# Moving the work between a kernel's stages into its attention loops: output projections, norms, router and gate products batch by batch

## What is computed

```python
x = x + tanh(g_xattn[0]) * L0_xattn(ctx, layernorm(x))   # 8 heads of 64; keys and values from ctx and from x; then Wo
x = x + tanh(g_ffn[0])   * L0_ffn(layernorm(x))          # router, top 2 of 8 experts of 256-1024-256, plus a shared one
x = x + tanh(g_xattn[1]) * L1_xattn(layernorm(x), ctx)   # 16 heads of 16; then Wo and its bias
x = x + tanh(g_ffn[1])   * L1_ffn(layernorm(x))          # gate over 16 experts, their q, k, v mixed into one head,
                                                         # causal attention inside a batch, 16 output projections
```

## Time and profile before

| what | us |
|---|---|
| median of 3 runs (lowest, highest) | 980.82 (979.62, 981.01) |
| the profiled execution, its own time | 984.02 |
| its span, first to last instruction | 982.2 |

### The profile page before, as it was taken

The page is one execution under the profiler, slowest core; times in us unless marked ns, Lnnn a source line. Parts: engine busy times, 40 slices in busy tenths (PEclk is TensorE's granted clock), DMA queues, the critical chain, the costliest instruction groups (busy, mean ns, idle before and its releaser), DMA issues.

```text
span 982.2 us, 14323 instructions
## 1 busy us (share of the span) xinstructions
PE 877.5 (89%) x5152; PEld 619.1 (63%) x5152; DVE 482.8 (49%) x1136; ACT 337.8 (34%) x907; POOL 145.8 (15%) x202
## 2 busy tenths in 40 slices
PE   0699999999997799999999988999999966699978
PEld 0555465555645666699889966667776646355557
DVE  3467666756663331013223248466666651666631
ACT  1244344434434121133322323566666611011110
POOL 3221022022000006000000046122233002000000
PEclk9999999999999789899999998999999975799979
DMA  7400001300000635156555333100000000000001
GB/s 218 160 16 1 16 17 28 102 0 2 1 1 1 207 135 171 50 171 218 190 192 166 114 105 119 82 2 2 2 1 2 2 1 1 0 1 0 0 5 33
DMA packets 37413, 62.21 MB, mean 63 GB/s; under 512 B 4595, under 2 KB 28924, under 8 KB 37092
## 3 DMA queue, kind: packets, MB, share of 16 engines
q1 hardware_dynamic: 35812, 57.68, 17.5%
q0 software_dynamic: 1536, 3.67, 1.2%
HBM read 53.08 MB, written 8.26 MB: 62 GB/s over the span
## 4 chain that ended last, share of the span: by engine, by line
PE 74%; DVE 9%; issue 6%; DMA 5%; ACT 2%; POOL 2%; SPq 1%; ACTq 0%; POOLq 0%; DVEq 0%
PE ps L1480 9%; PE ps L1397 8%; PE ps L1098 7%; PE ps L1158 6%; PE ps L1309 6%; PE ps L1147 5%; PE ps L1144 5%; PE ps L1321 5%; PE ps L1221 5%; DMA OT<-slot_rows 3%; PE ps L1131 3%; PE ps L1178 3%; PE ps L1255 3%; PE ps L1244 3%; PE ps L1419 2%
## 5 line engine op out<-in xcount | busy, mean ns | idle before, releaser
L766 DVE TENSOR_REDUCE negmax<-ps 112x1 f32<-112x375 f32 (+1 forms) x192 | 112.8, 587 | 125.0 <-PE ps L1158 62.5
L1098 PEld LDWEIGHTS ps<-ident,arena 112*125 112x125 f32 (+5 forms) x776 | 106.4, 164 | 91.3 <-issue 44.6
L1098 PE MATMUL ps<-ident,arena 112*125 112x112 f32 (+5 forms) x776 | 115.8, 267 | 23.2 <-POOL arena L380 18.2
L1480 PE MATMUL ps<-arena 128*112 128x384 f32 x256 | 91.3, 501 | 12.8 <-DVE arena L1024 12.8
L637 ACT ACTIVATE arena<-ps,negmax 112x375 f32<-112x375 f32 x128 | 73.5, 574 | 58.0 <-DVE negmax L766 58.0
L609 ACT ACTIVATE OT<-ps,bt 128x128 f32<-128x128 f32 x168 | 48.0, 368 | 113.5 <-PE ps L1309 112.6
L1309 PE MATMUL ps<-OT,arena 128*128 128x128 f32 x672 | 80.9, 280 | 0.2 <-DVE OT L874 0.2
L1309 PEld LDWEIGHTS ps<-OT,arena 128*128 128x128 f32 x672 | 79.2, 197 | 0.6 <-issue 0.6
L1321 PE MATMUL ps<-arena,OT 128*128 128x256 f32 x336 | 75.8, 379 | 0.0
L1158 PE MATMUL ps<-arena 128*112 128x487 f32 x128 | 65.9, 598 | 7.0 <-issue 5.1
L534 ACT ACTIVATE arena<-ps,negmax 112x487 f32<-112x487 f32 x64 | 42.7, 667 | 82.7 <-DVE negmax L766 82.6
(11 more groups left out here) (219 smaller groups left out, 1247.2 us busy)
## 6 DMA issues: line engine op xcount, KB each, us to landing
arena<-in_up_w SPq DMA_DIRECT2D x21, 1024.0 KB, 5.1
arena<-in_down_w SPq DMA_DIRECT2D x8, 1024.0 KB, 11.3
arena<-in_wqkv SPq DMA_DIRECT2D x1, 3072.0 KB, 12.5
arena<-in_ctx SPq DMA_DIRECT2D x8, 375.0 KB
slot_rows<-acc SPq DMA_DIRECT2D x3, 896.0 KB, 9.4
OT<-slot_rows SPq DMA_DIRECT2D x21, 128.0 KB, 4.9
slot_out<-yo SPq DMA_DIRECT2D x21, 128.0 KB, 1.7
wbuf<-in_ctxT SPq DMA_DIRECT2D x5, 375.0 KB, 5.3
```

Source lines behind the costliest of these rows:

```text
L766: dve.tensor_reduce(negmax[0:TQ, h % 2:h % 2 + 1], ps[0:TQ, h % 2, 0:n], AX, ALU.max, negate=True)\
L1098: return pe.transpose(dst, src, ident[0:k, 0:k])
L1480: ins = pe.matmul(ps[0:TQ, g % 4, 0:384], xb[p][:, c, :], wqkv[:, c, 2 * g:2 * g + 2, :].rearrange("p e n -> p (e n)"), start=(c == 0), st ...
```

## The change

In both cross-attentions the work that stood between the stages is now done batch by batch inside the loop, one or two batches behind the attention.

- **First loop.** PE: projection of batch n-1 at head 5 (`l0_o`), transposes of n-2 at head 1 (`l0_x`), router product of n-2 at head 4 (`l0_r`). DVE: residual and statistics of n-1 at head 6, norm of n-2 at head 0, logits of n-2 at head 4. POOL: the inverse root of one batch, between `ctx_norm` and `latents`. ACT: copy at head 1, exponential of the logits at head 5. The new jobs take their turn in banks 5 to 7; the order is written out by `l0_sequence`, and `l0_bank_free` waits for the copy of the job three places before. What is left after the loop (batches 6 and 7) is set between the first units of the shared expert. ACT's order there is `l0_x(6)`, gelu 0, `l0_ot(7)`, exponential 6, gelu 1, `l0_x(7)`, exponential 7, gelu 2.
- **Second loop.** PE: projection of n-1 at head 7 (`l1_o`), transposes of n-1 at head 14 (`l1_x`), gate products of n-2 at head 1 (`l1_g`), all in bank 5. DVE: logits of n-2 out of PSUM at head 2, rows of n-1 at head 9, norm at head 12. ACT: copy and square at head 14. The gate of batches 0 to 4 is made in batch 7, in five parts at heads 3, 5, 7, 11 and 14, and that of batches 5 to 7 in the last feed-forward, between the mixes of batches 1 and 2. `xsq` and `g1` move to other buffers.
- **Last feed-forward.** The loops over batches are written out. The projections of four batches stand between the steps of the last chain (`f_out`), the other four after it.

The core of the diff, indented less here:

```diff
+g1 = acc[:, :, :].rearrange("p t d -> p (t d)").rearrange("p (k n) -> p k n", k=16)
+xsq = wbuf0[:, 2048:2048 + KC * TOK].rearrange("p (c q) -> p c q", c=KC)
...
+    for n in range(B):
+        if n + 2 < B:
+            ctx_norm(n + 2, n % 2)
+        if n:
+            rows_rstd(n - 1)
+        if n + 2 < B:
+            latents(n + 2, n % 2)
...
     spread(0)
+    spread(1)
+    q_heads(1)
     for n in range(1, B):
-        spread(n)
-        q_heads(n)
...
+    f_rows(0)
+    f_rows(1)
+    rows_rstd1(B - 1)
+    norms(B, GA, B)
+    for n in range(2, B):
+        f_rows(n)
...
     def l0_batch(n, p, nxt):
         for h in range(H0):
             l0_exp(n, h)
+            if n >= 2 and h == 1:
+                l0_x(n - 2)
+            if n >= 2 and h == 5:
+                l0_r(n - 2)
+            if n == 0 and h == 6:
+                act.wait_ge(s_small, 16 * N_SMALL)
+                act.activation(tgate[:, :], gate[:, :], ACT.Tanh).then_inc(s_tanh, 1)
+                act.activation(sgate[:, :], gates[:, :], ACT.Exp, scale=-1.0).then_inc(s_sge, 1)
...
         l0_batch(n, n % 2, n + 1 < B)
     l0_pt(8 * H0 - 2)
     l0_pt(8 * H0 - 1)
-    l0_ot(7)
-    act.wait_ge(s_small, 16 * N_SMALL)
...
-    act.wait_ge(s_rz, 1)
-    act.activation(rt[:, 1, :], rt[:, 0, :], ACT.Exp, scale=-1.0).then_inc(s_rexp, 1)
-    for u in range(FM):
+    l0_x(6)
+    sh_gelu(0)
+    l0_ot(7)
+    l0_r(6)
+    sh_gelu(1)
+    l0_x(7)
+    l0_r(7)
...
+    def l1_x(n):
+        act.wait_ge(s_xt, 3 * B + n + 1)
+        act.activation(xnT[:, :, n * TQ:(n + 1) * TQ], ps[:, 5, 0:KC * TQ].rearrange("p (c q) -> p c q", c=KC),
+                       ACT.Copy).then_inc(s_xte, 1)
+        act.wait_ge(s_xte, 3 * B + n + 1)
+        act.activation(xsq[:, :, n * TQ:(n + 1) * TQ], xnT[:, :, n * TQ:(n + 1) * TQ], ACT.Square)\
+           .then_inc(s_sq1, 1)
...
     for n in range(B):
         l1_batch(n)
     l1_pt(8 * H1 - 2)
-    xnT_out(3, None, None)
...
+    def l0_rows(n):
+        if n == 0:
+            dve.wait_ge(s_tanh, 1)
+        dve.wait_ge(s_op, n + 1)
+        dve.scalar_tensor_tensor(x[:, n, :], ps[0:TQ, l0_bank("o", n, 0), 0:D], tgate[0:TQ, 0:1], x[:, n, :],
...
+        dve.wait_ge(s_res, n + 1)
+        link(dve.bn_stats(st6[:, n, :], x[:, n, :]))
+        dve.bn_aggr(mv[:, n, :], st6[:, n, :]).then_inc(s_bstat, 1)
...
+    def l0_norm(n):
+        dve.wait_ge(s_brstd, n + 1)
+        dve.tensor_scalar(xn[:, n, :], x[:, n, :], mv[:, n, 0:1], rstd[:, n:n + 1], ALU.subtract, ALU.mult)\
+           .then_inc(s_xn, 1)
...
+            if n >= 2 and h == 4:
+                l0_logits(n - 2)
             if nxt and h >= 4:
                 l0_k(n + 1, 1 - p, h - 4)
             if h >= 1 or positive(n):
                 softmax_norm(L0, n * H0 + h - 1, (h - 1) % 8, probs, NKP0)
             if stats and h == 2:
                 ctx_stats(n + 2, p)
+            if n >= 2 and h == 0:
+                l0_norm(n - 2)
+            if n and h == 6:
+                l0_rows(n - 1)
     for m in range(4):
         l0_k(0, 0, m)
     for n in range(B):
         l0_batch(n, n % 2, n + 1 < B, n + 2 < B)
...
+    l0_logits(6)
+    l0_rows(7)
+    l0_norm(7)
+    l0_logits(7)
     def bc(v, n):
...
+    def l1_rows(n):
+        dve.wait_ge(s_op, B + n + 1)
+        link(dve.tensor_tensor(xn[:, n, :], ps[0:TQ, 5, 0:D], bo[0:TQ, :], ALU.add))
+        dve.scalar_tensor_tensor(x[:, n, :], xn[:, n, :], tgate[0:TQ, 1:2], x[:, n, :], ALU.mult, ALU.add)\
+           .then_inc(s_res1, 1)
+        dve.wait_ge(s_res1, n + 1)
+        link(dve.bn_stats(st6[:, n, :], x[:, n, :]))
+        dve.bn_aggr(mv[:, n, :], st6[:, n, :]).then_inc(s_stat1, 1)
+    def l1_norm(n):
+        dve.wait_ge(s_rstd1, n + 1)
+        dve.tensor_scalar(xn[:, n, :], x[:, n, :], mv[:, n, 0:1], rstd[:, n:n + 1], ALU.subtract, ALU.mult)\
+           .then_inc(s_xn, 1)
+    def l1_logits(n):
+        dve.wait_ge(s_glog, n + 1)
+        if n == 0:
+            dve.tensor_copy(n2[:, B:], ps[0:TQ, 5, 32:32 + E1])
+        dve.tensor_copy(n2[:, n:n + 1], ps[0:TQ, 5, E1:E1 + 1])
+        dve.tensor_copy(g1[:, 0, n * E1:(n + 1) * E1], ps[0:TQ, 5, 0:E1]).then_inc(s_glogd, 1)
...
+    def gate_const():
+        dve.wait_ge(s_sge, 1)
+        dve.wait_ge(s_gpow, 1)
+        dve.tensor_scalar(sgate[:, :], sgate[:, :], 1.0, None, ALU.add)
...
+    def gate_part(part, lo, hi):
+        m = hi - lo
...
+        if part == 2:
+            link(dve.scalar_tensor_tensor(gr(6), gr(4), -8.0, gr(0), ALU.mult, ALU.add))
+            first_largest(gv(6), E1, gv(7), gv(8), io16, gs[:, 2, lo:hi], None, gs[:, 3, lo:hi])
+        if part == 3:
+            link(dve.tensor_tensor(gr(9), gr(4), gr(7), ALU.add))
+            link(dve.tensor_scalar(gs[:, 4, lo:hi], gs[:, 0, lo:hi], 0.0, None, ALU.is_le))
+            link(dve.tensor_tensor(gv(9), gv(9), bc(gs[:, 4, lo:hi], E1), ALU.mult))
...
+            if n >= 2 and h == 2:
+                l1_logits(n - 2)
+            if n == 4 and h == 3:
+                gate_const()
+            if n == 7 and h in (3, 5, 7, 11, 14):
+                gate_part((3, 5, 7, 11, 14).index(h), 0, GA)
+            if n and h == 9:
+                l1_rows(n - 1)
+            if n and h == 12:
+                l1_norm(n - 1)
     l1_q(0, 0)
     for n in range(B):
...
+    l1_logits(6)
+    f_mix(0, 0, 0)
+    l1_rows(7)
+    for g in range(1, 4):
         f_mix(0, 0, g)
-    for g in range(8):
-        f_mix(1, 1, g)
-        f_att(0, 0, g)
-    with dve.Fori(0, 3) as i:
-        for p in (0, 1):
-            n = i * 2 + 2 + p
-            for g in range(8):
-                f_mix(n, p, g)
-                f_att(n - 1, 1 - p, g)
+    l1_norm(7)
+    for g in range(4, 8):
+        f_mix(0, 0, g)
+    for n in range(1, B):
+        for g in range(8):
+            f_mix(n, n % 2, g)
+            if n == 1 and g == 0:
+                l1_logits(7)
+            f_att(n - 1, (n - 1) % 2, g)
+            if n == 1 and g in (3, 5, 7):
+                gate_part((g - 3) // 2, GA, B)
+            if n == 2 and g in (1, 3):
+                gate_part(3 + g // 2, GA, B)
     for g in range(8):
         f_att(7, 1, g)
-    for t in range(B):
-        dve.wait_ge(s_op, 2 * B + t + 1)
-        dve.scalar_tensor_tensor(x[:, t, :], ps[0:TQ, t, 0:D], tgate[0:TQ, 3:4], x[:, t, :], ALU.mult, ALU.add)\
-           .then_inc(s_y, 1)
+        if g in (2, 3, 5):
+            f_out((2, 3, 5).index(g))
+    for t in range(3, B):
+        f_out(t)
...
+    def l0_bank_free(kind, n, j):
+        i = L0_SEQ.index((kind, n, j))
+        if i >= 3:
+            was, m, k = L0_SEQ[i - 3]
+            if was == "o":
+                pe.wait_ge(s_res, m + 1)
+            elif was == "x":
+                pe.wait_ge(s_xte, B + m + 1)
+            elif was == "r":
+                pe.wait_ge(s_rz, m + 1)
+            else:
+                pe.wait_ge(L0[was + "e"], m * L0_PER[was] + k + 1)
+        return 5 + i % 3
...
+    def l0_o(n):
+        pe.wait_ge(L0["ote"], n + 1)
+        bank = l0_bank_free("o", n, 0)
+        for c in range(4):
+            ins = pe.matmul(ps[0:TQ, bank, 0:D], ot0[:, n % 2, c, :], wo[:, c, :], start=(c == 0), stop=(c == 3))
+        ins.then_inc(s_op, 1)
...
             if nxt:
                 if h == 2:
                     l0_t1(n + 1, 1 - p)
                 if h == 3:
                     l0_q(n + 1, 1 - p)
-                if h >= 4:
-                    l0_kv(n + 1, 1 - p, h - 4)
+            if n >= 2 and h == 4:
+                l0_r(n - 2)
+            if nxt and h >= 4:
+                l0_kv(n + 1, 1 - p, h - 4)
+            if n and h == 5:
+                l0_o(n - 1)
             if h >= 2 or n:
                 l0_pt(n * H0 + h - 2, (h - 2) % 8)
...
+    l0_pt(8 * H0 - 2, 6)
+    l0_pt(8 * H0 - 1, 7)
+    l0_x(6)
     pe.wait_ge(s_shw, 32)
-    for u in range(2 * FM):
+    pe.wait_ge(L0["exp"], B * H0)
+    sh_up(0)
+    l0_pv(7, 6)
+    l0_r(6)
+    sh_up(1)
+    l0_o(7)
+    pe.wait_ge(L0["pte"], B * H0)
+    sh_down(0)
+    sh_up(2)
+    l0_x(7)
+    sh_down(1)
+    l0_r(7)
+    for u in range(3, 2 * FM):
         sh_up(u)
-        if u:
-            sh_down(u - 1)
...
+    def l1_g(n):
+        pe.wait_ge(s_sq1, n + 1)
...
+            pe.matmul(ps[0:TQ, 5, 0:E1], xnT[:, c, n * TQ:(n + 1) * TQ], simm[:, c, :], start=(c == 0),
...
+        for c in range(KC):
+            ins = pe.matmul(ps[0:TQ, 5, E1:E1 + 1], xsq[:, c, n * TQ:(n + 1) * TQ], ones[:, 0:1], start=(c == 0),
...
             l1_s(n, p, h)
+            if n >= 2 and h == 1:
+                l1_g(n - 2)
             if nxt and h == 4:
                 l1_q(n + 1)
+            if n and h == 7:
+                l1_o(n - 1)
+            if n and h == 14:
+                l1_x(n - 1)
             if h >= 2 or n:
...
+    l1_g(6)
+    pe.wait_ge(s_pta, 8 * B)
+    pe.wait_ge(s_ptv, 8 * B)
+    pe.wait_ge(L1["exp"], B * H1)
     pe.wait_ge(s_wF, 32)
...
+    def f_out(t):
+        pe.wait_ge(s_mte, t + 1)
```

(61 more changed lines are left out.)

293 lines of the change are left out of this document (154 added, 139 removed).

## The result

The changed kernel takes 935.5 us (median of 4 runs, 934.9 to 939.0), the kernel before 980.9 (4 runs): ratio 0.955, 95% interval 0.952 to 0.957. A later set of runs gave 936.6 to 979.8, ratio 0.956 (0.954 to 0.958). The forecast was 938 us.

The account below looks back on a forecast made before the run. PE bounds the kernel, full inside both attention loops but idle or slow-clocked between stages. Gains of 12.5 + 21.4 + 8.4 = 42.3 us off the 980.82 median give 938 us, range 927 to 952.

Parts of the forecast that it names:

- First junction: Between first attention loop and shared expert: removing PE's 30.9 us hole, less returned work and stalls, gains 12.5 us (8 to 16).
- table loads on the path: ACT switching between exponential and gelu at the first loop's end: 2.0 us of exposed stall (0 to 5.1).
- Second junction: Between second attention loop and last feed-forward: removing 48.1 us, less 16.0 of PE work and 16.0 of stalls, gains 21.4 us.
- The stalls: Second loop and last stage: PE waits for added DVE and ACT work, 16.0 us in all.
- Rows at head 9: Second loop, DVE's 1.6 us of rows behind an odd head: 0.9 us stall per batch, seven times, 6.3 (2 to 11).
- the slack of 0.7 us: Second loop: a DVE piece behind an odd head delays the two-head cycle by its length less about 0.7 us.
- filled waits of the scores' weight loads: Second loop: weight loads wait 7.6 us for the exponential; added PE work there is free, 4.0 us credited (0 to 7.6).
- The end: Last feed-forward: late projections of 3.45 us cover the last chain's waits, 37.9 us becoming 29.5, gain 8.4 (7 to 9).
- Nothing stalls: Both loops: added DVE and ACT pieces find room, most stalls come back, 921 us; chance 0.06.
- DVE bounds: Second loop: DVE becomes the bound, all stall bounds hold, 32.6 us instead of 16.0, giving 955 us; chance 0.09.
- The norms wait for POOL: Second loop, head 12: DVE's norms blocked by POOL's instructions, seven times, 28 us, giving 966 us; chance 0.05.
- The loop falls to 1.2 GHz: Small gate or router products inside the loops pull PE's clock down; 1002 us with three slow batches; chance 0.04.

Follow-up runs that it names:

- the best version: Changed kernel with second-loop rows cut in two, gate spread out, ScalarE reordered at the shared expert, and two pieces of DVE gate work moved: 925.9 us, ratio 0.944.

## Why the prediction was right

**The method** held: junctions are worth their holes plus the slow clock around them, less PE work counted by instruction. Right for the reasons given, with stall terms too dear and one credit that did not come. That these nearly cancel is luck.

**First junction, 12.5 said, 12.9 found.** A batch of the first loop takes 36.56 us (said 36 to 36.5; before 33.92). Two terms were off, in opposite senses. The table loads on the path were given 2.0 us and cost 0.84; four of the five loads lay beside PE work. And 2.3 us of batch 7's idle time were to be filled; batch 7 now starts 14.4 us later, so the stretch that answers to the old one begins at 309.4:

```profile
309.40:327.80 18.40, 14.74 (x122) 9.92 (x121) 9.86 (x28) 9.52 (x25) 0.79 (x2) 1.00 0.01 2
```

PE still idles 3.7 us there, so 1.5 of the 5.2 was filled. With 1.2 more for the loads and 0.8 less for the filling the sum is 12.9; that it meets the 12.9 found is luck, since 0.8 of that lies before the first scores. ScalarE's copy, 1.4, left no idle of its own in the full batches of the loop, but a batch grew by 2.64 us where its PE work was priced at 2.4, so the 0.2 a batch may stand in that.

**Second junction, 21.4 said, 23.8 found.** PE's part was nearly right: 16.0 us over eight batches is 2.0 each, measured 1.87. The stalls, 16.0 us, were in fact 10.5, of which:

- Rows at head 9: 0.9 per batch said, 0.53 found. What was mis-sized is the slack of 0.7 us read from two heads. It is an idle time of DVE, and says how long DVE waits for PE, not how late DVE may be before PE waits. The measured cushion is larger: of 1.5 us of rows PE paid 0.5. Probably PE's projection at head 7 and the value products between are what widens it; no run separates these.
- ScalarE's copy and square at head 14: 2.8 said, nothing found; no idle of PE stands there.
- The gate's constants: 1.2 said, 0.40 found, with two of the instructions 0.44 and 0.50 us long beside POOL instead of 0.16 and 0.17.
- The gate in batch 7: 5.0 said, 4.2 found.
- The last stage: 0.7 said; its idles are 0.50, 0.33 and 1.39, 2.2 in all. I had counted DVE's free third there and not asked what the long third piece stands in front of, the mask and maximum of the attention chain.

Against this, the 4.0 us credited as filled waits of the scores' weight loads did not come. The waits of the second loop afterwards (total, times, longest):

```profile
PEld ps L1558 <- ACT arena L688: 15.3, 35, 1.9
PE ps L1558 <- ACT arena L688: 7.0, 11, 1.7
PEld ps L1558 <- issue: 4.2, 24, 0.3
```

The issue waits are what they were, 4.1 and 4.2. These loads run ahead of PE, so their waits were no hole: between 626.7 and 790 us of the kernel before no idle of PE itself was longer than 0.1 us. 21.4 + 5.5 - 4.0 = 22.9. The last 0.9 is about what PE's part came out below its price, 8 x (2.0 - 1.87) = 1.0, if all batches are like the measured one. The 23.8 hold a half-clock spell; with the undisturbed loop of 190.4 us the junction gives 25.3.

**The end, 8.4 said, 8.2 found**, and 8.8 came back when it was undone.

**The sum.** Stages that the change does not touch made the gap between the profile's gain (48.7) and the median's (45.5). I had taken off 3.2 us for it, since the profile of before lay that far over its median, and the experts' 3.9 us are that much.

**The rivals.** *Nothing stalls* is nearly what spreading the gate and the rows made of it, and the best version's 926 lies toward that rival's 921. *DVE bounds* falls: every stall of the loop came out below its forecast, and spread thin the same DVE work left no idle. *The norms wait for POOL*: all eight took 403 to 405 ns. POOL was idle beside seven of them, as argued; beside one it was at its power, which held nothing up. Its mechanism is real and struck where I had not looked. *The loop falls to 1.2 GHz* falls: the clock was 1.00 up to batch 7 with the small products at head 1.
